# Route weights repeated over the expert rows by DMA instead of by selector products, with two PSUM banks for the gate products, in a two-layer attention and mixture-of-experts kernel

## What is computed

```python
# layer 0: T = 1024 tokens a batch, H = 128, M = 64, E = 16 experts, top 2, and one shared expert
shared = jax.nn.silu(x @ ws_gate) * (x @ ws_up) @ ws_down
scores = jax.nn.sigmoid(x @ gate_w.T)
topk_w, topk_idx = jax.lax.top_k(scores, 2)
topk_w = topk_w / (topk_w.sum(-1, keepdims=True) + 1e-20) * 2.5
route = jnp.zeros((T, E)).at[jnp.arange(T)[:, None], topk_idx].set(topk_w)
g = jnp.einsum('th,ehm->etm', x, w_gate)
u = jnp.einsum('th,ehm->etm', x, w_up)
eo = jnp.einsum('etm,emh->eth', jax.nn.silu(g) * u, w_down)
routed = jnp.einsum('te,eth->th', route, eo)
return routed + shared
```

## Time and profile before

| what | value |
|---|---|
| median of 3 runs | 2198.44 us (2196.4 to 2199.55) |
| the profiled execution | 2198.01 us, of which the span of the instructions is 2196.2 us |
| TensorE busy | 2063.4 us, 94% of the span, 12072 matmul instructions |
| VectorE, ScalarE, GpSimd busy | 71%, 55%, 6% |
| chain that ended last | 86% TensorE, 7% VectorE, 3% ScalarE, 1% DMA |
| DMA queues | 71.75 MB, 12.2% of 16 engines' time |

### The profile page before, as it was taken

One profiled execution on the slowest core, in us unless ns is written; L12 is line 12 of the kernel. 1 busy time (PEld: TensorE's weight loads), 2 busy tenths in 40 slices (PEclk: granted clock), 3 DMA queues, 4 the chain that ended last, 5 costly groups with the idle time before them and its releaser, 6 DMA issues.

```text
span 2196.2 us, 33681 instructions
## 1 busy us (share of the span) xinstructions
PE 2063.4 (94%) x12072; PEld 956.6 (44%) x12072; DVE 1559.4 (71%) x2854; ACT 1216.3 (55%) x2329; POOL 130.4 (6%) x251
## 2 busy tenths in 40 slices
PE   5968999999999999998999999999999999999889
PEld 3621233335755323343666423333475532334355
DVE  5667787755679788673778888775567978877154
ACT  1323677775341667777342367777534166777721
POOL 2000001100000001110000000110000000111000
PEclk9956999999999999999999999999999999999989
DMA  4060100100041110100004110010004111010000
GB/s 155 1 172 1 30 16 26 31 2 1 1 115 39 30 30 23 33 16 2 1 26 114 44 30 16 26 31 3 1 1 116 32 37 30 16 30 17 1 0 10
DMA packets 46983, 71.75 MB, mean 33 GB/s; under 512 B 7968, under 2 KB 17120, under 8 KB 46432
## 3 DMA queue, kind: packets, MB, share of 16 engines
q1 hardware_dynamic: 46816, 69.61, 12.2%
HBM read 46.25 MB, written 22.54 MB: 31 GB/s over the span
## 4 chain that ended last, share of the span: by engine, by line
PE 86%; DVE 7%; ACT 3%; issue 2%; DMA 1%; SPq 1%; POOL 0%; DVEq 0%; ACTq 0%
PE ps L1543 18%; PE ps L1518 16%; PE ps L1487 16%; PE ps L1409 8%; PE ps L1386 8%; PE ps L1419 7%; DVE row_max L1038 3%; PE ps L1553 2%; PE ps L1338 1%; PE ps L1326 1%; ACT prob L1232 1%; PE ps L1307 1%; PE ps L1520 1%; PE ps L1332 1%; PE ps L1437 1%
## 5 line engine op out<-in xcount | busy, mean ns | idle before, releaser
L1232 ACT ACTIVATE prob<-ps 128x512 f32<-128x512 f32 (+3 forms) x1792 | 864.9, 555 | 351.2 <-PE ps L1518 262.7
L1038 DVE TENSOR_REDUCE row_max<-ps 128x1 f32<-128x1024 f32 x512 | 604.6, 1219 | 104.0 <-PE ps L1487 103.4
L1518 PE MATMUL ps<-q_stack,k_stack 96*128 96x512 bf16 (+4 forms) x1792 | 552.0, 364 | 30.6 <-ACT prob L1232 17.2
L1487 PE MATMUL ps<-k_stack,q_stack 96*128 96x512 bf16 (+4 forms) x1792 | 531.4, 370 | 22.9 <-DVE row_max L1038 13.4
L1035 DVE CUSTOM_DVE_ANT_0 tmp<-ps,const_b 128x128 f32<-128x128 f32 (+7 forms) x512 | 371.7, 756 | 131.3 <-PE ps L1487 117.9
L1543 PE MATMUL ps<-prob,v_ones 128*32 128x512 f32 (+3 forms) x3584 | 438.9, 562 | 2.2 <-ACT prob L1232 2.2
L1518 PEld LDWEIGHTS ps<-q_stack,k_stack 96*128 96x128 bf16 (+1 forms) x1792 | 172.6, 98 | 354.6 <-ACT prob L1232 224.2
L1487 PEld LDWEIGHTS ps<-k_stack,q_stack 96*128 96x128 bf16 (+1 forms) x1792 | 149.7, 99 | 383.1 <-DVE row_max L1035 93.3
L1175 ACT ACTIVATE prob<-ps 128x512 f32<-128x512 f32 x128 | 76.4, 597 | 295.6 <-PE ps L1409 295.5
L1386 PEld LDWEIGHTS ps<-wd,prob 128*128 128x128 f32 (+1 forms) x1600 | 207.1, 191 | 59.4 <-issue 39.1
L1386 PE MATMUL ps<-wd,prob 128*128 128x128 f32 (+1 forms) x1600 | 212.9, 276 | 4.1 <-DVE prob L943 4.1
(11 more groups left out here) (178 smaller groups left out, 1546.1 us busy)
## 6 DMA issues: line engine op xcount, KB each, us to landing
k_stack<-scratch_k SPq DMA_DIRECT2D x48, 256.0 KB, 6.4
q_stack<-scratch_q SPq DMA_DIRECT2D x48, 256.0 KB, 7.1
scratch_k<-tmp SPq DMA_DIRECT2D x36, 256.0 KB, 2.6
k_stack<-scratch_k SPq DMA_DIRECT2D x96, 64.0 KB, 2.2
q_stack<-scratch_q SPq DMA_DIRECT2D x96, 64.0 KB, 2.2
scratch_k<-tmp SPq DMA_DIRECT2D x36, 128.0 KB, 2.4
scratch_q<-tmp SPq DMA_DIRECT2D x12, 256.0 KB, 2.4
xx<-in_x SPq DMA_DIRECT2D x4, 512.0 KB, 4.3
```

The costliest lines, as they stand in the source:

```text
L1038: dve.tensor_reduce(nm[G % 2][:, t, j:j + 1], ring_pair(r)[:], AX_X, ALU.max).then_inc(s["ring_used"], 1)
L1232: act.activation(p_slot(v, j)[:, lo - at:hi - at], bank(UNIT_BANKS[u % 3])[:, 0:hi - lo], ACT.Exp, scale=SCALES[kind_of(G)]).then_inc(s["p ...
L1487: ins = pe.matmul(ring_pair(r)[:, lo:hi], queries(G, j)[:, t * P:(t + 1) * P], keys(G, j)[:, lo:hi], start=True, stop=True)
L1518: ins = pe.matmul(dst[:, 0:hi - lo], keys(G, j)[:, kc * P:(kc + 1) * P], queries(G, j)[:, lo:hi], start=True, stop=True)
```

## The change

The route weights stay fp32 and whole. They are turned by eight fp32 transposes, copied to `routeT` (16 or 8 rows), stored to a scratch tensor in HBM (`routes_out`), and read back with one row repeated over 64 or 128 partitions (`spread_in`) into one of four SBUF buffers `spread_w`. One load serves one step of mixture (b, 0) (two DMAs, an expert each) and two steps of mixture (b, 1) (one DMA): 16 loads of 256 KB for every mixture, 128 in all. VectorE reads `spread_w` where it read PSUM. A load waits until the step that last read its buffer has been multiplied. The shared expert's steps, whose weight is 1, have no product: the up product's result goes straight to `hid`. The bank that comes free becomes the second gate bank, used in turn. For layer 0 of batches 1 to 3 the transposes, the copy (on VectorE), the store and the first four loads are strewn into the window; for batch 0 they and the routing itself come after the wait for the weights. For layer 1 the transposes go to `XA`, after the output projection (batches 0 to 2) or before it (batch 3). The two PSUM pairs of the pieces swap their turns. The constants `sel0` and `sel1` (2112 bf16 columns) are no longer loaded.

The core of the diff:

```diff
+LOADS_OF = 16
+SPREADS = 4
-PAIRS = (3, 2)
+PAIRS = (2, 3)
-    cb = np.concatenate([np.eye(P), mask_wide, sel0, sel1], axis=1)
+    cb = np.concatenate([np.eye(P), mask_wide], axis=1)
...
-                at = do("PE", "gate", 0.88, last(taken), last(scaled), last(ups), xT if n == 0 else None, *(freed if n == 0 else ()))
+                at = do("PE", "gate", 0.88, last(taken, 2), last(taken) if n == 1 else None, last(scaled, 2), last(ups), xT if n == 0 else None, *(freed if n == 0 else ()))
...
-    for item in front(0):
+    for item in front(0)[:FRONT_FIRST.index("route0")]:
         plan.put(*item)
     plan.add("weights")
...
-        G_BANK, U_BANK, Y_BANK, SPREAD_BANK = 0, 1, 2, 3
+        G_BANKS, U_BANK, Y_BANK = (0, 3), 1, 2
...
+            def routes_out(b, which):
+                if which == 0:
+                    sp.wait_ge(s["ring_used"], ROUTES_RING[b] + 1)
+                else:
+                    sp.wait_ge(s["rt_ready"], b + 1)
+                if b:
+                    sp.wait_ge(s["hid_ready"], plan.step0[b - 1, which] + 2 * CHUNKS[which])
+                sp.dma_start(scratch_r[which], routeT[0:EXPERTS[which], :]).then_inc(s["routes_stored"], 16)
+
+            def spread_in(load):
+                (b, which), i = plan.mixtures[load // LOADS_OF], load % LOADS_OF
+                half, c = divmod(i, LOADS_OF // 2)
+                dst, tok = spread_w[load % SPREADS], slice(half * HALF, (half + 1) * HALF)
+                sp.wait_ge(s["routes_stored"], 16 * (routed_before(b, which) + 1))
+                if load >= SPREADS:
+                    sp.wait_ge(s["hid_ready"], LAST_STEP[load - SPREADS] + 1)
+                if which == 1:
+                    sp.dma_start(dst[:], scratch_r[1][c, tok].partition_broadcast(P)).then_inc(spread_loaded[load % SPREADS], 16)
+                else:
+                    for n in range(2):
+                        sp.dma_start(dst[M0 * n:M0 * (n + 1), :], scratch_r[0][2 * c + n, tok].partition_broadcast(M0)).then_inc(spread_loaded[load % SPREADS], 16)
...
-                        st.done(dve.scalar_tensor_tensor(left, key, scale, wide(col(6)), ALU.mult, ALU.mult))
-                        st.wait()
-                        for part in range(PARTS):
-                            dst = rt[which][:, :, part, 0:experts]
-                            ins = dve.tensor_copy(dst, left)
...
+                        dst = routes[which][:].rearrange("p (t e) -> p t e", e=experts)
+                        dve.scalar_tensor_tensor(dst, key, scale, wide(col(6)), ALU.mult, ALU.mult).then_inc(s[("route_ready0", "route_ready1")[which]], 1)
...
-                dve.wait_ge(s["spread_psum"], spread_count(b, which, n))
+                if load is None:
+                    dve.wait_ge(s["hid_ready"], k)
+                    dve.sem_inc(s["hid_ready"], 1)
+                    return
+                dve.wait_ge(spread_loaded[load % SPREADS], spread_count(load))
                 if k >= 2:
                     dve.wait_ge(s["down_done"], k - 1)
-                dve.tensor_tensor(hid[k % 2][0:m, :], gu[k % 2][0:m, :], bank(SPREAD_BANK)[0:m, :], ALU.mult).then_inc(s["hid_ready"], 1)
+                dve.tensor_tensor(hid[k % 2][:], gu[k % 2][:], spread_w[load % SPREADS][:], ALU.mult).then_inc(s["hid_ready"], 1)
...
-                dst = bank(SPREAD_BANK).bitcast(BF16)
+            def turn_routes(dst, which):
                 for t in range(T):
-                    ins = pe.transpose(dst[0:PARTS * CW, t * P:(t + 1) * P], routes[which][:, t * PARTS * CW:(t + 1) * PARTS * CW], ident_b)
+                    ins = pe.transpose(dst[0:EXPERTS[which], t * P:(t + 1) * P], routes[which][:, t * EXPERTS[which]:(t + 1) * EXPERTS[which]], ident_f)
...
-                if which == 0 and n:
-                    pe.wait_ge(s["g_used"], 2 * C0 * b + n)
-                elif n:
-                    pe.wait_ge(s["sg_ready"], k)
+                if n == 1 and plan.evacuated_then[b, which]:
+                    pe.wait_ge(s["o_evac"], plan.evacuated_then[b, which])
+                if which == 0 and n >= 2:
+                    pe.wait_ge(s["g_used"], 2 * C0 * b + n - 1)
+                elif n >= 2:
+                    pe.wait_ge(s["sg_ready"], k - 1)
...
+                elif stage == "turn_r":
+                    pe.wait_ge(s["route_ready1"], b + 1)
+                    if b < B - 1:
+                        pe.wait_ge(s["po_used"], b + 1)
+                    turn_routes(XA, 1).then_inc(s["rt_psum"], 1)
                 elif stage == "turn_h":
                     pe.wait_ge(s["shift1_ready"], b + 1)
+                    if b == B - 1:
+                        pe.wait_ge(s["rt_ready"], b + 1)
```

226 lines of the change are left out of this document (121 added, 105 removed).

## The result

The changed kernel takes 2203.69 us (median of 20 runs, 2198.65 to 2211.81), the kernel before 2199.17 (20 runs, 2195.87 to 2201.96). Ratio 1.0025, 95% interval 1.0018 to 1.0032: slower by 4.5 us, where 27 less were predicted. The profiled execution has a span of 2198.2 us against 2196.2.

The account below looks back on a forecast made before the run. The prediction took TensorE's instruction stream to bound the kernel. Its terms, -29.9 + 3.6 - 5.9 + 3.0 + 1.9 = -27.3, taken from 2198.0 us gave 2171 us, range 2160 to 2186.

Parts of the forecast that it names:

- The start: Batch 0's opening: earlier w_down scaling and fewer constant loads, less two new waits, gain 5.9 us; bounds -11 and 0.
- The starts of the mixtures (0..2, 1): Where these mixtures open: tighter order makes transposes and xn's turn wait, +1 us each, +3 us; bounds -1 and +4 each.
- The wait for the first stack of q: Where the pieces begin in the dense stretches: the sum has no term for a wait there.
- The third rival: VectorE's longer chains cost +4 at three mixture starts and the start gives nothing: 2186 us, chance 0.12.
- Each lies in a stretch that TensorE fills, so 136 x 0.22 = -29.9: All mixtures: removing 136 selector products takes 0.22 us each from TensorE's full stream, -29.9 us.
- products were not the limit: Stretches' ends: a wait for maxima or stacks takes up the gap, 2195 us or more, chance 0.03.
- The bound of nothing: All stretches: were VectorE or a wait the next limit, nothing of the removed products' 29.9 us would come through.
- clock falls in the new waits: Round the fp32 transposes: steps behind the waits run at the lower clock, 4 us in three stretches, 2183, chance 0.07.
- The windows: Four windows: fp32 transposes cost 0.45 us more per turned set of routes, three sets lying there, +1.4 us.
- The last stretch: Last mixture: uncovered store and load path makes first down 2.8 us later, +1.9 us; bounds 0 and +5.
- Loads at nothing: Later spread_w loads in the mixtures: four buffers cover them, 3.1 us expected alone, cost nothing.
- loads come late: Mixtures (b, 0): loads above 4.1 us run the four buffers dry; at 4.6 us, 2203 us, chance 0.06.

Follow-up runs that it names:

- e3: Kernel before without its 136 selector products, VectorE multiplying by a fixed SBUF operand, order unchanged: 2187.03 us, ratio 0.9950.
- e9: Changed kernel with only the next batch's front-stage items put back to their earlier places in the windows, gate 1's wait kept: 2195.31 us, ratio 0.9977.
- e5: e2 with the next batch's front stages at their earlier window places and the six new items behind the last unit: 2164.17 us, ratio 0.9853.
- e8: e5 with 128 bf16 products of 128x512 put back ahead of the up products, nothing reading them: 2193.82 us, ratio 0.9981.
- e6: e2 with one gate bank in place of two, and planned for one: 2194.37 us, ratio 0.9981.
- e11: Changed kernel with 20 unread bf16 products filling TensorE's idle time ahead of gate 1's wait in three dense stretches: 2194.04 us, ratio 0.9980.
- e2: e1 with the planner's dependency of gate 1 on gate 0's reader dropped as well: 2181.01 us, ratio 0.9927.
- e1: Changed kernel, same order, with gate 1 no longer waiting for VectorE's up product of step 0: 2188.19 us, ratio 0.9959.
- e4: Changed kernel without its 192 spread_w transfers, a constant in the four tiles: 2201.19 us, ratio 1.0016.
- e10: e5 without its 192 spread_w transfers, a constant in the four tiles: 2165.29 us, ratio 0.9843.

## Why the prediction was wrong

**The start (-5.9, with its 18 products -9.4): right in size, its make-up not shown.** The first unit comes 8.9 us earlier, the first down starts at 40.51 (predicted 40.4; the terms of that sum add up to 40.7). The first gate starts at 27.57, not near 24, because encoding goes first; that is order, and the sum had its work. But at the last gate of the mixture (100.5 before, 94.4 now) only 6.1 us are gained, the other 2.8 arise behind it, where the sum had nothing, and the 18 products alone brought 0.3 (e3). So some luck is in the agreement.

**The starts of the mixtures (0..2, 1), +1 us each: the step that failed.** It counted no wait for VectorE at gate 1, since "a second gate bank lets TensorE run on". The bank is there, but the wait at n = 1 was not relaxed, and 4.93 us stand where 0.8 + 1.4 were counted. It could be read in the code and in the order: gate 1 ahead of the transposes, VectorE's up product of step 0 behind normalising. The bound of +4 for each was also too low, since it had no clock. From the first gate of (0, 1) to the first unit, 601:723 before and 589:717 after, 5.8 us were lost where the terms make -2. Freeing the gate brings 13.6 us, with its plan 20.7: the largest part found of the 31.8 us between forecast and result. It doesn't decide the sign alone: with only the late items spaced as before (e9) the kernel also ends below the kernel before (-3.1).

**The wait for the first stack of q, put at nothing.** The third rival notes that "the pieces start earlier between the steps", and the sum counts nothing for it. They now start before the stack has landed: 2.33, 2.38 and 2.20 us in the three dense stretches, none before. No run takes this wait out.

**"Each lies in a stretch that TensorE fills, so 136 x 0.22 = -29.9": wrong of the kernel before, but not where the 31.8 us went.** In the changed kernel mixture (1, 0) gained 4.1 us for 18 products, and with both faults mended (e5) the whole change brings 34.9, 7.6 more than forecast. What was wrong is the ground given for it. The price is right in the last mixture, and as what leaves TensorE's stream, but "fills" was read off busy shares of 96 to 100%, and these do not show short waits: a gate's row says 1.02 us when the next matmul starts 0.86 later, and 1.13 when it starts 0.96 later. The Trainium skill ("Perfetto Trace Analysis", section on identifying the most-contended engine) says that the busy time of matmuls is a poor measure of how near the limit a kernel is. The traces agree: e3 is 95% busy in 598:720 and lost 16 products there without a gain. They differ on the reason: the page has pipelined instructions look smaller in the trace, and here the 1.02 us of a gate are longer than its 0.86 in the stream. Taken out of the kernel before they brought 10.2 (e3), part of the rest being clock. That the price comes through in the new order (e8) owes much to the second gate bank with its plan, worth about 12 us (e6), a gain that the sum did not name; that the 29.9 could stand is in that measure luck. The rival *products were not the limit* had 0.03 because it was thought of as a wait at the stretches' ends; in e3 it is short waits between the steps, for VectorE's row maxima in the one shown. The bound of nothing was named and then set aside with "VectorE has 20 us free": a mean over 121 us, which says nothing of a piece that waits for its slot.

**The rival *clock falls in the new waits* (0.07, +12) is what happened, on top.** Its argument against was the place of before, a wait of 0.99 at a granted 1.00; but the wait is five times as long. e11 prices it at 9.0 by the medians. The mean granted clock of the profiled executions is 0.971 before, 0.962 after and 0.971 in e5. Between two levels, 1.2 and 2.4 GHz, a mean of 0.962 is 2 x 0.038 x 2198 = 167 us at the lower one and 0.971 is 127: an estimate of 40 us more, worth up to 20 if TensorE works through them. The prediction weighed for this rival what the Trainium skill says in "TensorE: Matmul & The Clock Gate", part on the PE-mode transpose: that transposes don't count as TensorE being busy the way products do. No run here needs it: gate 1, ahead of the transposes, already takes 2.04 us, so TensorE's standing still ahead of them is enough, and filling that wait brought the gate back to 1.12 us with the transposes unchanged.

**The windows (+1.4): the other large step.** The 0.45 for each turned set was right (1.04 us a set); that six more items in the same list move all the others was not thought of. Measured +6.7, and e5's windows are 11.4 shorter than e2's. Why it is that much was not taken apart beyond the places shown.

**The last stretch (+1.9): size and mechanism off.** +4.0, where -1.2 was the sum with its products. Counted from the last unit (2078.3 before, 2076.3 after), the sum had the store's issue at 28.0 and the first down at 34.7; they came at 30.7 and 38.8:

```profile
2107.04 0.28 SPq L749 DMA_DIRECT2D scratch_r<-routeT  x1
2108.83 7.89 SPq L759 DMA_DIRECT2D spread_w<-scratch_r  x5
```

```profile
2111.76 1.28 DVE L1180 SCALAR_TENSOR_TENSOR x<-ps,scale,x 128x1024 f32<-128x1024 f32 x1 [7.03 <-PE ps L1647]
2113.08 1.23 DVE L1183 TENSOR_TENSOR x<-x,bias_vo 128x1024 f32<-128x1024 f32 x1
2114.22 0.68 DVE L1019 TENSOR_TENSOR prob<-prob,spread_w 128x512 f32<-128x512 f32 x1
```

The store is late since the gates ahead run at the lower level until about 2104 (until about 2100 in the kernel before, whose stretch begins 2 us later), and gate 1 waits 0.93 us for VectorE there too; with that gate freed (e1) the stretch takes 118.5 us in place of 121.9. The store itself was cheaper than counted: the first load is issued 1.8 us after it, against 2.9. The 2.15 us that the prediction worked out from the Trainium skill ("DMA: Bandwidth & Descriptors", anatomy of one DMA) was nearer, though the page gives that figure for transfers issued by GpSimd and this one is SyncE's. The rest is not the path over DMA: the first load has landed by about 2112.3 (2108.83 and the median of 3.5), and the route product stands behind the projection's copy and bias in VectorE's order; e4 waits the same 3.33 us with no load at all.

**Loads at nothing: right within 2 us** (2.9 and 3.5 us to landing; e4 and e10). The rival *loads come late* gave 2203 and the result was 2203.69, by another cause.

With both faults mended the change does bring what it was made for: e5 is at 0.9853 (0.9835 to 0.9871) of before, 34.9 us, and in that kernel products of this size are worth their full price (e8).

## What to carry to other kernels

A small piece of work taken from a nearly full engine is worth its time only if no chain stands just below; leave it out of the kernel as it is, and double it, and the two numbers say how level the limits are, once the granted clock of both has been looked at. When a buffer is added, read every wait on the old one for its first uses (n = 0, 1), and tell the planner the waits that the code really has. Here a new wait of some microseconds on TensorE was paid twice, once standing and once at the lower clock, and a list that spaces work evenly moves all of it when items are added.

## What the runs showed of the hardware

- The same kernel's time goes with its granted clock: the changed kernel's 20 runs reach from 2198.65 us at 0.963 to 2211.81 at 0.958, e9's from 2182.2 at 0.970 to 2203.3 at 0.958.
- The level at one place varies between batches of one execution. The encoding that opens a dense stretch takes 1.8 us or 3.5 to its successor: in the six profiled kernels that open it with the encoding and space 18 late items evenly it was the long one at 12 of 18 places, in the six with the items moved at none of 18.
- A DRAM row of 2 KB read 128 times into 256 KB of SBUF landed in 3.5 us (median of 64). Other transfers of that size take 2.3 to 2.7 us (stores of q, k and the output) or 6.8 and 7.6 (stack loads) in the same trace. Leaving all of these loads out changed the time by less than 2 us by offset (e4, e10).
